# The result is stored in two parts, x's load follows both transposing DMAs, and its statistics come a tile later

## What is computed

```python
def layer(x, ctx):
    q, k, v = layernorm(x) @ Wq.T + bq, ctx @ Wk.T + bk, ctx @ Wv.T + bv
    x = x + softmax(q @ k.T / sqrt(128)) @ v
    h = layernorm(x)
    probs = softmax(h @ router_w.T)
    count = argmax(clip(gelu(h @ actor_w1.T + b1) @ actor_w2.T + b2, -30, 30)) + 1
    score = where(rank(probs) < count, probs, 0)
    for e in range(8):
        x = x + score[..., e:e+1] * ((silu(h @ gate_w[e].T) * (h @ up_w[e].T)) @ down_w[e].T)
    return x                      # 336 hidden units per expert
```

## Time and profile before

| | us |
|---|---|
| median of 3 runs | 762.27 (761.92 to 762.60) |
| profiled execution, whole time | 762.07 |
| profiled execution, span from first to last instruction | 760.3 |
| TensorE busy | 746.9 (98%) |
| VectorE busy | 630.6 (83%) |
| ScalarE busy | 557.9 (73%) |
| GpSimd busy | 580.9 (76%) |

### The profile page before, as it was taken

How to read it: one execution, slowest core, us unless ns; L and a number is a source line. 1 busy time by engine, 2 the same in 40 slices (tenths; PEclk the granted TensorE clock), 3 DMA queues, 4 the chain that set the end, 5 groups by cost and what they waited for, 6 DMA issues and landing times.

```text
span 760.3 us, 13864 instructions
## 1 busy us (share of the span) xinstructions
PE 746.9 (98%) x3765; PEld 370.7 (49%) x3765; DVE 630.6 (83%) x1384; ACT 557.9 (73%) x987; POOL 580.9 (76%) x618
## 2 busy tenths in 40 slices
PE   8999999999999999999999999999999999999998
PEld 4544454444445445454554545445454554544445
DVE  6899888887888889788888887889788887878877
ACT  5997777767778767777777778767777777777664
POOL 2587978879696886968689696886968688696863
PEclk9999999999999999999999999999999999999999
DMA  9110221303022140302313022140312412020110
GB/s 347 51 34 15 56 42 36 78 14 84 16 69 57 28 99 6 91 28 48 76 27 83 14 68 55 27 97 6 90 28 49 76 15 57 0 56 15 28 29 29
DMA packets 98046, 40.31 MB, mean 53 GB/s; under 512 B 66896, under 2 KB 93136, under 8 KB 98000
## 3 DMA queue, kind: packets, MB, share of 16 engines
q1 hardware_dynamic: 97712, 39.30, 21.5%
q10 hardware_dynamic: 288, 0.48, 0.2%
HBM read 24.01 MB, written 8.16 MB: 42 GB/s over the span
## 4 chain that ended last, share of the span: by engine, by line
PE 76%; POOL 8%; issue 7%; DVE 5%; ACT 2%; DMA 2%; SPq 0%; POOLq 0%; DVEq 0%; ACTq 0%
PE bank L567 23%; PE bank L569 23%; PE bank L568 23%; POOL weighted L1129 5%; PE bank L459 2%; PE bank L481 1%; PE bank L470 1%; PE bank L563 1%; DVE bank L1461 1%; DMA xn_lo<-xn_lo 1%; PE bank L525 1%; DVE hid_lo L1467 1%; ACT silu L898 1%; PE bank L544 1%; POOL v_early L1071 1%
## 5 line engine op out<-in xcount | busy, mean ns | idle before, releaser
L1129 POOL TENSOR_TENSOR weighted<-silu,score_bc 128x512 f32<-128x512 f32 x336 | 435.2, 1308 | 124.8 <-ACT silu L898 118.8
L1461 DVE SCALAR_TENSOR_TENSOR bank<-bank,h_scale,weighted 128x512 f32<-128x512 f32 x336 | 252.8, 752 | 84.6 <-PE bank L569 44.6
L892 ACT ACTIVATE hid_hi<-bank 128x512 f16<-128x512 f32 x336 | 200.5, 597 | 163.7 <-DVE bank L1461 160.7
L898 ACT ACTIVATE silu<-bank,silu_scale 128x512 f32<-128x512 f32 x336 | 230.4, 686 | 20.4 <-PE bank L569 20.0
L1467 DVE TENSOR_TENSOR hid_lo<-bank,hid_hi 128x512 f16<-128x512 f32 x336 | 227.9, 678 | 13.2 <-ACT hid_hi L892 13.2
L567 PE MATMUL bank<-xn_lo,up_hi 128*128 128x512 f16 x336 | 127.5, 379 | 2.3 <-DVE hid_lo L1467 2.3
L567 PE MATMUL bank<-xn_lo,gate_hi 128*128 128x512 f16 x336 | 127.5, 380 | 0.4 <-ACT silu L898 0.4
L569 PE MATMUL bank<-xn_hi,up_hi 128*128 128x512 f16 x336 | 127.3, 379 | 0.0
L568 PE MATMUL bank<-xn_hi,up_lo 128*128 128x512 f16 x336 | 127.3, 379 | 0.0
L569 PE MATMUL bank<-xn_hi,gate_hi 128*128 128x512 f16 x336 | 127.3, 379 | 0.0
L568 PE MATMUL bank<-xn_hi,gate_lo 128*128 128x512 f16 x336 | 127.3, 379 | 0.0
(11 more groups left out here) (195 smaller groups left out, 801.9 us busy)
## 6 DMA issues: line engine op xcount, KB each, us to landing
x_in<-in_x SPq DMA_DIRECT2D x16, 256.0 KB, 2.9
y_kept<-y_sb SPq DMA_DIRECT2D x60, 64.0 KB, 2.6
y_tok<-y_kept SPq DMA_DIRECT2D x15, 256.0 KB, 2.8
out<-out_sb SPq DMA_DIRECT2D x15, 256.0 KB, 2.4
xt_in<-in_x_t SPq DMA_DIRECT2D x14, 256.0 KB, 2.9
row_bc<-row_kept SPq DMA_DIRECT2D x14, 256.0 KB, 3.7
ctx_in<-in_ctx_t SPq DMA_DIRECT2D x14, 240.0 KB, 2.8
raw_gate<-in_gate_t SPq DMA_DIRECT2D x3, 448.0 KB, 6.1
```

The lines of the kernel that those rows point to most:

```text
L892: af(hid_hi[j % HRING][:], up_bank[j % U_BANKS][:], ACT.Copy).then_inc(hid_hi_ready, 1)
L898: af(silu[j % RING][:], gate_bank[(par + j) % G_BANKS][:], ACT.Silu, scale=silu_scale[:])\
L1129: g.tensor_tensor(weighted[j % RING][:], silu[j % RING][:], score_bc[par][:], ALU.mult)\
L1461: v.scalar_tensor_tensor(up_bank[j % U_BANKS][:], up_bank[j % U_BANKS][:], h_scale[:], weighted[j % RING][:], ALU.mult, ALU.mult).then_inc ...
```

## The change

The store of a block is issued in two parts, batches 0 to 2 at its old place (192 KB) and batch 3 (64 KB) after the wait for the low half. x's load moves behind the transposing DMA of the low half. `stats_1` moves from tile 4 to 5, `aggregate_1` from 5 to 6, `rstd_1` from 6 to 7; turn 0 keeps its places (8, 9 and 10). As each block now raises `stored` by 32, the waits on it are doubled.

```diff
+            def store(n, par, lo, hi):
+                sp.dma_start(out_blocks[n][:, lo:hi], out_sb[par][:, lo:hi]).then_inc(stored[par], 16)
...
                 if is_block(t - 2):
-                    sp.dma_start(out_blocks[t - 2], out_sb[par][:]).then_inc(stored[par], 16)
+                    store(t - 2, par, 0, BB - 1)
                 if by_dma:
                     turned(xn_hi[1 - par], xn2_hi).then_inc(halves_in[1 - par], 16)
                     sp.wait_ge(lo_ready, t + 2)
+                if is_block(t - 2):
+                    store(t - 2, par, BB - 1, BB)
+                if by_dma:
+                    turned(xn_lo[1 - par], xn2_lo).then_inc(halves_in[1 - par], 16)
                 if is_block(t + 3) and not (isinstance(t, int) and t == 0):
                     sp.dma_start(x_in[1 - par][:], x_blocks[t + 3]).then_inc(x_loaded[1 - par], 16)
-                if by_dma:
-                    turned(xn_lo[1 - par], xn2_lo).then_inc(halves_in[1 - par], 16)
...
             sp.wait_ge(half_ready, 1)
-            sp.dma_start(out_blocks[BLOCKS - 1][:, 0:2], out_sb[1][:, 0:2]).then_inc(stored[1], 16)
+            store(BLOCKS - 1, 1, 0, 2)
             sp.wait_ge(out_ready, BLOCKS)
-            sp.dma_start(out_blocks[BLOCKS - 1][:, 2:BB], out_sb[1][:, 2:BB]).then_inc(stored[1], 16)
-            sp.wait_ge(stored[0], 16 * (BLOCKS // 2))
-            sp.wait_ge(stored[1], 16 * (BLOCKS // 2 + 1))
+            store(BLOCKS - 1, 1, 2, BB)
+            for par in range(2):
+                sp.wait_ge(stored[par], 16 * BLOCKS)
...
-                    if j == 6 + 4 * late(t) and is_block(t + 3):
+                    if j == (10 if late(t) else 7) and is_block(t + 3):
                         rstd_1(t + 3, nxt)
...
-                    dve.wait_ge(stored[par], 8 * (n - par))
+                    dve.wait_ge(stored[par], 16 * (n - par))
...
-                dve.wait_ge(stored[1], 16 * (BLOCKS // 2 - 1))
+                dve.wait_ge(stored[1], 16 * (BLOCKS - 2))
...
-                    if j == 4 + 4 * late(t) and is_block(t + 3):
+                    if j == (8 if late(t) else 5) and is_block(t + 3):
                         stats_1(t + 3, nxt)
...
-                    if j == 5 + 4 * late(t) and is_block(t + 3):
+                    if j == (9 if late(t) else 6) and is_block(t + 3):
                         aggregate_1_waits(t + 3)
...
-                    if j == 5 + 4 * late(t) and is_block(t + 3):
+                    if j == (9 if late(t) else 6) and is_block(t + 3):
                         aggregate_1(t + 3)
```

## The result

| | before | after |
|---|---|---|
| median of 11 runs, us | 762.16 (761.75 to 762.82) | 764.07 (762.71 to 764.27) |
| ratio after / before | | 1.0022 (1.0014 to 1.0031) |
| profiled execution, us (span) | 762.07 (760.3) | 763.7 (761.9) |

The changed kernel is slower, by 1.9 us in the medians and 1.6 in the profiled executions. That lies outside the range. The difference is 0.2% of the time, small, but clear of the scatter: the interval of the ratio leaves out 1.

What follows compares the result with a forecast made beforehand. TensorE was taken to be the bound, losing 2.52 us at line 525 to waits for lo. Profiled 762.07 less a gain of 2.5 gives 759.6, plus 0.2 for the median 759.8; range 759.0 to 761.4.

Steps and rivals of the forecast that it cites:

- What bounds: TensorE, busy 98%, loses 2.52 us at line 525 in turns 1, 3 and 4 waiting for lo, a transposing DMA.
- (1) to (3): On SP, lo without x's load ahead lands in 2.5 us instead of 3.0, small store included; issue place kept.
- (4): At line 525, turns 1 to 4, 0.05 of 2.52 us lost stays, gain 2.5; turn 3's lo slips past the fetch.
- rival B: In turn 3 the fetch still catches lo, landing at 3.9; gain 1.2 to 1.5, time 760.8 to 761.1; chance 0.17.
- (5), (6): x lands about 4.1 us after lo's issue; its statistics at tile 5 on DVE cost nothing or some tenths.
- rival D: x lands late and holds DVE at tile 5; over 6 us, 12 turns pay, 765.8 at 6.5; chance 0.06.
- C: Small store delays lo, or TensorE waits for hid_lo instead; gain 0 to 1.2, time 761.1 to 762.3; chance 0.13.
- (7): Aggregates and POOL's rstd_1 one tile later: a slip of some tenths at tiles 7 to 9 swallowed by 3.68 us idle.
- (8): SP's stored row for the next block 2 us later, the last turn's extra store and doubled semaphore counts cost nothing.

Runs made afterwards that it cites:

- experiment 5: The changed kernel with only the statistics later: aggregates in the same tile 5, rstd_1 back at tile 6, row_top in SBUF; 761.18 us.
- Experiment 9: The changed kernel with row_top in PSUM from block 2 on, and 63 more waits in TensorE's stream in turn 2; 759.70 us.
- Experiments 1 and 4: 1: the changed kernel with statistics, aggregates and rstd_1 back at tiles 4, 5 and 6, 766.27 us; 4: the same with row_top in PSUM, 761.96 us.

## Why the prediction was wrong, by its steps

**What bounds (right).** TensorE's losses at line 525 were 2.5 us, and a lost microsecond wasn't made up: the differences between the traces only add up.

**(1) to (3), lo's landing and the small store (right).** Where no fetch meets it, lo lands in 2.4 to 2.5, against the 2.5 taken. The small store lands in 1.5 us, not the estimated 2.15, and costs lo nothing to be seen; its issue is 0.34 where I took 0.38, and lo was issued at 88.89 in turn 1, against 88.88.

**(4), the losses (right in two turns of three).** Turns 1 and 4 gained 0.37 and 0.54, as worked out. Turn 3 gained 0.60, not 1.6. I read correctly that a fetch holds up lo, and then let lo slip past it. Two things are wrong with that. The fetch's moment isn't fixed: it came 1.2 us earlier (180.48 to 179.29), while lo's issue moved by 0.09. And lo would not have slipped past it at its old distance either: in experiment 5 the fetch stood 2.29 us after lo's issue, with all of lo's data ahead of it, and lo landed at 4.3, not 2.5. That its data is ahead of the fetch doesn't bring lo past it. This is rival B, at its price: lo landed at 3.9 us, as B said, and the gain at line 525 was 1.51, B's upper end. The trace of before had a second case, which the prediction doesn't mention: lo of turn 12 landed in 4.0 us, with a smaller fetch (8 KB) 2.1 us after its issue. Experiment 9 is the other half, 0.9 us more by medians once turn 3's fetch is elsewhere, with the overlap of intervals said there.

**(5), (6), x and its statistics (right).** x landed 3.8 us after its issue in turn 3, where DVE's cover held, and nothing of it reached TensorE. Experiments 1 and 4 show what rival D would have been: a wait for x at tile 4 that costs 1.4 us in sum by medians. D as written, at tile 5, didn't happen. C didn't either: hid_lo's entry is 2.6, not 2.3 plus the gain.

**(7), aggregates and `rstd_1` a tile later (wrong, and what put the time outside the range).** I priced it at nothing, as POOL stood idle for 3.68 us afterwards. Two things fail in this sentence. That idle time lies at tile 12, behind row_bias and behind ACT's first table load, so it is no cover for what happens at tiles 7 to 9. And I asked only whether POOL's work would be late, not which DVE instruction it would then stand beside. With `rstd_1` (1.9 us on POOL, 324.22 to 326.10) between two products instead of ahead of both, the second ends at 327.33 instead of 326.84, and row_bias starts inside it. It cost 3.1 us, where no rival had a term: 759.8 became 760.8 by B, still within the range, and with 3.1 it is 763.9. The measured median is 764.07.

The trace of before could have said so. In turn 2 its row_bias takes 0.47 us instead of 0.15, and ends with POOL:

```profile
142.76 2.50 POOL L1129 TENSOR_TENSOR weighted<-silu,score_bc 128x512 f32<-128x512 f32 x2
...
144.81 0.47 DVE L1322 SCALAR_TENSOR_TENSOR row_bias<-row_top,rstd 128x4 f32<-128x4 f32 x1
```

Fourteen equal instructions of 4 columns, twelve of them 0.15 us long, one 0.32 (turn 1) and one 0.47, are a lock seen from the side.

**(8), the later row and the doubled counts (right).** Nobody waits for them in any trace.

## What to carry to other kernels

When work is moved on GpSimd by a tile, list each VectorE instruction with two operands in SBUF that runs near the old and the new place: a tiny one can be held until GpSimd's large product ends, and what exceeds the gap behind it is lost. An idle stretch covers a slip only if it lies ahead of the first reader. One operand of such an instruction put into PSUM takes the lock away without moving anything, and a repeated 0.26 us shows best from start to start at one line, turn by turn, while the list of waits hides it. And a transfer is past a disturbance only when it has landed: its last data being through isn't enough.

## What the runs showed of the hardware

- A DVE instruction of 128x4 with two operands in SBUF took 0.15 us alone and 0.75 beside a POOL product of 1.27, ending with it within 0.02 us; with one operand in PSUM it took 0.15 inside the same product.
- An instruction fetch of one packet of 0.02 MB, 1.0 to 2.7 us after the issue of a transposing DMA, put 0.9 to 1.9 us on its landing (2.5 to between 3.4 and 4.3; with x's load ahead 3.0 to between 4.5 and 4.8), though it takes only one of 16 DMA engines; the landing came 1.0 to 1.6 us after the fetch's end. In experiment 5 all of lo's data and 30 of 32 counts were through before the fetch started, and it landed at 4.3. A fetch of 8 KB 0.8 us after the issue cost nothing (turn 1, 2.44), one 2.1 us after it went with 4.0 (turn 12 of before). By the Trainium skill, DMA: Bandwidth & Descriptors, "Queues, rings and completion order", a completion count lands only after every earlier write of that DMA engine, across its queues; the traces agree (the two late counts of experiment 5 come as the fetch ends), but they don't name the DMA engine of a packet, so that this is the reason isn't shown.
- The fetch's moment differs by over a microsecond between kernels with the same TensorE instructions (180.48 and 179.29).
- A store of 64 KB landed 1.5 us after its issue, one of 192 KB after 2.2, and a transposing DMA issued 0.38 us behind the first was not slowed.
